# A decoder layer's attention stage on one core: a new order of steps, loads in two parts, the second norm moved and rewritten, four unread products at the seam

## The reference

```
# 1 attention with relative positions (16 heads of 8), per batch
q, k, v = x @ Wq + bq, x @ Wk + bk, x @ Wv + bv
scores  = (q k^T + c2p(q, pos_k) + p2c(k, pos_q)) / sqrt(3 * 8)
a       = softmax(scores) v @ Wo + bo
x       = layernorm(a + x) * ln_scale + ln_bias      # "first norm", eps 1e-7
# residual and a post norm around it
x       = layernorm(x_in + x)                        # "second norm", eps 1e-5
# 2 cross attention to ctx_768 (ternary weights, int8 activations), then a norm
# 3 four rounds of four experts (128 -> 512 -> 128, top 2 of 4)
# 4 a last norm
```

## Time and profile before

| | |
|---|---|
| median of 3 runs | 2843.77 us (2837.84 to 2845.44) |
| the profiled execution | 2838.59 us, of which its span 2836.9 us |
| busy over the span | PE 2414.7, DVE 2232.0, ACT 2286.8, POOL 711.7 us |
| attention stage | from 0 to about 950 us of the span |
| one body of its loop | 54.70 us |
| mean granted clock of TensorE | 0.939 of 2.4 GHz |

### The profile page before, as it was taken

One profiled execution on the slowest core, in us unless ns is written; L12 is line 12 of the kernel. 1 busy time (PEld: TensorE's weight loads), 2 busy tenths in 40 slices (PEclk: granted clock), 3 DMA queues, 4 the chain that ended last, 5 costly groups with the idle time before them and its releaser, 6 DMA issues. The chain is left out here.

```text
span 2836.9 us, 64292 instructions
## 1 busy us (share of the span) xinstructions
PE 2414.7 (85%) x18180; PEld 1323.1 (47%) x18199; DVE 2232.0 (79%) x6591; ACT 2286.8 (81%) x4255; POOL 711.7 (25%) x565
## 2 busy tenths in 40 slices
PE   2888888888888337746699999999999999999997
PEld 1555555555555226614344444444444444444443
DVE  3788888788888576785488888888888888888887
ACT  1888888888888353317699999999999999999997
POOL 2334534544444101124311111111111111111114
PEclk7899999999999659977799999999999999999999
DMA  2000000000000100000011111211111121111113
GB/s 78 13 22 12 11 17 16 11 13 20 11 11 12 44 0 1 0 30 0 16 45 53 52 45 45 60 45 45 52 52 45 45 60 45 45 53 51 45 45 89
DMA packets 182540, 96.04 MB, mean 34 GB/s; under 512 B 22539, under 2 KB 179291, under 8 KB 182491
## 3 DMA queue, kind: packets, MB, share of 16 engines
q1 hardware_dynamic: 182491, 95.45, 12.0%
HBM read 78.10 MB, written 4.73 MB: 29 GB/s over the span
## 5 line engine op out<-in xcount | busy, mean ns | idle before, releaser
L1955 DVE TENSOR_TENSOR c_Hl<-c_HF,c_Hh 128x512 f16<-128x512 f32 x1028 | 679.6, 688 | 160.9 <-ACT c_Hh L1842 144.7
L1838 ACT ACTIVATE c_HF<-c_H,c_b 128x512 f32<-128x512 f32 x1028 | 711.0, 692 | 64.2 <-PE c_H L1777 44.3
L1842 ACT ACTIVATE c_Hh<-c_H,c_b 128x512 f16<-128x512 f32 x1028 | 706.4, 687 | 0.0
L1893 POOL TENSOR_TENSOR c_EX<-c_euler,c_D 128x16 f32<-128x16 f32 x65 | 188.6, 2902 | 1194.6 <-DVE c_D L1928 1194.6
L1775 PE MATMUL c_H<-c_Ch,SH 128*128 128x512 f16 x1028 | 390.1, 379 | 0.0
L1777 PE MATMUL c_H<-c_Ch,SH 128*128 128x512 f16 x1028 | 390.0, 379 | 0.0
L1776 PE MATMUL c_H<-c_Cl,SH 128*128 128x512 f16 x1028 | 390.0, 379 | 0.0
L1786 PE MATMUL c_Y<-c_Hh,SH 128*128 128x512 f16 x1024 | 388.1, 379 | 0.3 <-DVE c_Hl L1955 0.3
L1788 PE MATMUL c_Y<-c_Hl,SH 128*128 128x512 f16 x1024 | 388.1, 379 | 0.0
L1787 PE MATMUL c_Y<-c_Hh,SH 128*128 128x512 f16 x1024 | 388.1, 379 | 0.0
L692 DVE CUSTOM_DVE_ANT_0 a_T<-a_S,a_POS 128x128 f32<-128x128 f32 x1024 | 234.8, 285 | 48.0 <-PE a_S L436 41.0
(11 more groups left out here) (300 smaller groups left out, 4372.8 us busy)
## 6 DMA issues: line engine op xcount, KB each, us to landing
c_CWB<-c_rows SPq DMA_DIRECT2D x260, 256.0 KB, 4.1
a_QN<-a_QH SPq DMA_DIRECT2D x128, 32.0 KB, 1.9
a_KN<-a_KH SPq DMA_DIRECT2D x128, 32.0 KB, 1.8
out<-d_O SPq DMA_DIRECT2D x16, 256.0 KB, 2.3
a_QN<-a_QL SPq DMA_DIRECT2D x64, 32.0 KB, 1.9
a_KN<-a_KL SPq DMA_DIRECT2D x64, 32.0 KB, 1.8
CUR<-in_ctx SPq DMA_DIRECT2D x1, 1848.0 KB
c_rows<-c_CWR SPq DMA_DIRECT2D x65, 8.0 KB, 1.4
```

Source lines behind the costliest of these rows:

```text
L1838: act.activation(HF[:, k % 4, :], bH[k % 4][:, :], ACT.Gelu_apprx_tanh, bias=b1[:, g % EXPERTS, f:f + 1], scale=1.0 / WSCALE).then_inc(hf_ ...
L1842: act.activation(Hh[:, g % 2, f, :], bH[k % 4][:, :], ACT.Gelu_apprx_tanh, bias=b1[:, g % EXPERTS, f:f + 1], scale=1.0 / WSCALE).then_inc( ...
L1955: dve.tensor_tensor(Hl[:, g % 2, f, :], HF[:, k % 4, :], Hh[:, g % 2, f, :], ALU.subtract)\
```

## The change

- Loads: x comes in three parts. The first block is on a semaphore of its own (`x_in`), SP waits for it, then come the second block, the late loads and the rest of x (`late_in`). The engines start on the early loads alone. Five of GpSimd's fills move behind its first copy (`filled`).
- The stacking DMAs signal by group: `qn_in` and `kn_in` become four semaphores each, and a bucket tile waits for its own group. Who needs all of them waits for four.
- Steps: Q stays in step 1, K goes to step 2, with `high_half` behind the exponentials and `low_half` in steps 2 and 3. V's four products go to steps 10 to 13, one each, its sum to step 14. Tile 0 goes to step 5 and tile 1 stays in step 6 (`tiles_of`).
- `unit_columns` comes ahead of the tiles' roundings on ScalarE.
- GpSimd takes the maximum of units 7 to 13 and no longer of unit 6. `residuals` waits for the first norm of the block before instead of for its second.
- The second norm goes from step 9 to step 14, and from `tensor_scalar` with two columns to `scalar_tensor_tensor`, whose second tensor is the column rstd with a step of zero.
- In the last step TensorE does four products of 128 x 512 into bO that nobody reads.

```diff
-NORM_STEPS = (2, 3, 4, 5, 6, 7, 9)
+NORM_STEPS = (2, 3, 4, 5, 6, 7, 14)
+TILE_STEPS = (5, 6, 7, 7, 8, 8, 9, 9, 10, 10, 11, 11, 12, 12, 13, 13)
+V_STEPS = (10, 11, 12, 13)
-EARLY_MAX = range(6, 14)
+EARLY_MAX = range(7, 14)
+def tiles_of(u):
+    return [n for n, step in enumerate(TILE_STEPS) if step == u]
...
-        qn_in, kn_in = Count(sem("qn_in"), 16 * 3 * NG), Count(sem("kn_in"), 16 * 3 * NG)
+        qn_in, kn_in = ([Count(sem(n + str(g)), 16 * 3) for g in range(NG)] for n in ("qn_in", "kn_in"))
...
-                for src, dst in loads + late:
+                for src, dst in loads:
                     sp.dma_start(dst, src).then_inc(loaded, 16)
+                for n in range(2):
+                    sp.dma_start(X[:, n * NB:(n + 1) * NB, :], tokens[:, n * NB:(n + 1) * NB, :]).then_inc(x_in, 16)
+                    if n == 0:
+                        sp.wait_ge(x_in, 16)
+                for src, dst in late:
+                    sp.dma_start(dst, src).then_inc(late_in, 16)
...
-            def residuals(i):
-                hold(pool, spare_pool, link_s.sem, link_s.at(i, 0))
+            def residuals(i, first):
+                if not first:
+                    hold(pool, spare_pool, link_s.sem, link_s.at(i, -3))
...
-                if n == 0:
-                    pe.wait_ge(qn_in.sem, qn_in.at(i, qn_in.per * (1 + nxt)))
-                if n == 2 * NG:
-                    pe.wait_ge(kn_in.sem, kn_in.at(i, kn_in.per * (1 + nxt)))
+                if j == 0:
+                    done = (qn_in, kn_in)[kind][g]
+                    pe.wait_ge(done.sem, done.at(i, done.per * (1 + nxt)))
...
                     if u == 1 and not last:
-                        project_qk(i, 1)
+                        project_q(i, 1)
                     if u == 2 and not last:
-                        project_v(i, 1)
+                        project_k()
+                    if u in V_STEPS and not last:
+                        project_v(V_STEPS.index(u))
...
+                    if u == UNITS + TAIL - 1 and not last:
+                        for _ in range(4):
+                            pe.matmul(bO[:, :], window[:, 0:P], table[:, 0, :, :, :].rearrange("p k j n -> p (k j n)"),
+                                      start=True, stop=True)
...
                     if 0 <= u - 3 < UNITS:
                         exp_columns(i, u - 3)
-                    for n in range(2 * (u - 6), 2 * (u - 6) + 2):
-                        if 0 <= n < TILES and not last:
-                            high_rows(i, 1, n)
                     if u >= 7 and (u - 7) % UPB == 0 and u < 7 + UNITS:
                         unit_columns(i, (u - 7) // UPB)
+                    for n in tiles_of(u):
+                        if not last:
+                            high_rows(i, 1, n)
                     if u < UNITS:
                         exponentials(i, u)
+                    if u in (1, 2) and not last:
+                        high_half(i, 1, u - 1)
...
-                    last = dve.tensor_scalar(X[:, bass.ds(i * NB + b, 1), :], R[:, b, :], mv[:, b, 0:1],
-                                             rstd[:, b:b + 1], ALU.subtract, ALU.mult)
+                    last = dve.scalar_tensor_tensor(
+                        X[:, bass.ds(i * NB + b, 1), :].rearrange("p a h -> p (a h)"), R[:, b, :], mv[:, b, 0:1],
+                        rstd[:, b:b + 1].to_broadcast([P, H]), ALU.subtract, ALU.mult)
...
-                    if u == 1 and not last:
-                        low_half(i, 1, 0)
-                        low_half(i, 1, 1)
-                    if u == 2 and not last:
+                    if u in (2, 3) and not last:
+                        low_half(i, 1, u - 2)
+                    if u == 14 and not last:
                         values_in(i, 1)
```

More of the change, by code:

```diff
@@ L333, in _ @@
             const(pool.memset(PS, 0.0))
[L334 to L338, removed]
             const(pool.memset(half[:, :], -0.5))
             assert n == CONSTS
-            pool.wait_ge(loaded, LOADS)
+            pool.wait_ge(x_in, 16)
             copy_block(0, 0)
+            pool.wait_ge(xb.sem, 1)
+            pool.memset(table[96:128, :, :, :, :], 0.0).then_inc(filled, 1)
+            pool.wait_ge(filled, 1)
+            pool.memset(QN[96:128, :, :, :], 1.0).then_inc(filled, 1)
+            pool.wait_ge(filled, 2)
+            pool.memset(KN[96:128, :, :, :], 1.0).then_inc(filled, 1)
+            pool.wait_ge(filled, 3)
+            pool.memset(V[:, :, :, :], 0.0).then_inc(filled, 1)
+            pool.wait_ge(filled, 4)
+            pool.memset(V[:, :, :, DH:DH + 1], 1.0).then_inc(filled, 1)
+            pool.wait_ge(filled, FILLS)
             pool.wait_ge(built, BUILT)
@@ L363, in body @@
                         take_max(i, u)
-                    if u == NORM_STEPS[5] and not first:
-                        power(i - 1, 1)
-                residuals(i)
+                    if u in (NORM_STEPS[1], NORM_STEPS[5]) and not first:
+                        power(i - 1, (NORM_STEPS[1], NORM_STEPS[5]).index(u))
+                residuals(i, first)
                 if not last:
@@ L386, in transposes, with project_q, project_k, project_v @@
                 last.then_inc(xT_ps.sem, 1)
-            def project_qk(i, nxt):
+            def project_q(i, nxt):
                 pe.wait_ge(xT_ok.sem, xT_ok.at(i, 1 + nxt))
                 pe.matmul(bG[0][:, :], Wq[:, :], xT[:, ::-1, :], start=True, stop=True).then_inc(qk_ps.sem, 1)
+            def project_k():
                 pe.matmul(bG[1][:, :], Wk[:, :], xT[:, :, :], start=True, stop=True).then_inc(qk_ps.sem, 1)
[L393 to L396, removed]
+            def project_v(b):
+                pe.matmul(bM[:, b * S:(b + 1) * S], xT[:, :, b], Wv[:, :], start=True, stop=True).then_inc(v_ps.sem, 1)
             def bucket_tile(i, nxt, n):
@@ L500, in _ @@
             pe.wait_ge(tab, 5)
-            project_qk(0, 0)
-            project_v(0, 0)
+            project_q(0, 0)
+            project_k()
+            for b in range(NB):
+                project_v(b)
             pe.wait_ge(tab, TAB)
@@ L626, in body @@
                         x_columns(i, 1)
-                    if u == 1 and not last:
-                        high_half(i, 1, 0)
-                        high_half(i, 1, 1)
                     if 0 <= u - 3 < UNITS:
                         exp_columns(i, u - 3)
-                    for n in range(2 * (u - 6), 2 * (u - 6) + 2):
-                        if 0 <= n < TILES and not last:
-                            high_rows(i, 1, n)
                     if u >= 7 and (u - 7) % UPB == 0 and u < 7 + UNITS:
                         unit_columns(i, (u - 7) // UPB)
+                    for n in tiles_of(u):
+                        if not last:
+                            high_rows(i, 1, n)
                     if u < UNITS:
                         exponentials(i, u)
+                    if u in (1, 2) and not last:
+                        high_half(i, 1, u - 1)
                     if u in OUT_COLS:
@@ L868, in body @@
                         norm_step(i - 1, NORM_STEPS.index(u))
-                    for k in range(2 * (u - 6), 2 * (u - 6) + 2):
-                        if 0 <= k < TILES and not last:
+                    for k in tiles_of(u):
+                        if not last:
                             split_rows(i, 1, k)
```

53 lines of the change are left out of this document (31 added, 22 removed).

## The result

The changed kernel is slower: 2872.66 us median (2870.77 to 2873.83, 4 runs) against 2844.47 us (2837.84 to 2845.44, 4 runs), a ratio of 1.0104 (95% interval 1.0086 to 1.0121). The forecast was 2793. Of the profiled execution the span is 2870.8 us, 33.9 longer than before.

What follows compares the result with a forecast made beforehand. Waits between TensorE, VectorE and ScalarE, none full, make a body's time; the prologue waits for loads. Gains 22.0 (prologue) + 28 (14 bodies) + 1 - 3 = 48 us give 2793 us, own range 2776 to 2810, for all 2774 to 2830.

Steps and rivals of the forecast that it cites:

- second rival: Step 14: GpSimd gets between the norm's instructions; one turn 2819 us (chance 0.20), two 2845 (0.05), three 2867 (0.15).
- Loads, 16.3 us: Prologue: engines wait only for early loads and x's first 256 KB; start moves from 26.14 to about 9.8 us.
- Stacking by groups, 5.7 us: Prologue: with a semaphore for each group the first bucket tile starts at 49.4, not 55.15; 5.7 us gained.
- Fills, 0: Prologue: GpSimd's five fills behind the first copy end near 19 us, well before their reader; no cost counted.
- Clock, 1.0 us a body: Seam between bodies: four unread products keep TensorE's clock up, gaining 1.0 us a body, bounds 0 and 1.2.
- Q, K and V, 1.3 us: Steps 1 to 3: VectorE loses the wait for V's products and their sum; 1.3 us gained, bounds 0.8 and 1.8.
- V's pairs, -0.5: Steps 10 to 13: V's products return as one pair a step; 0.5 us a body lost, bounds 0 and 1.5.
- Step 9, 1.1 us: Step 9: the second norm's 2.11 us leave, then ScalarE sets the pace; 1.1 us gained, bounds 0.6 and 2.
- Bank's copy, 0: Step 12: the copy ahead of the roundings releases TensorE but delays those roundings; 0, bounds -0.5 and +0.5.
- Step 14, -0.9 us: Step 14 takes in the values' sum and second norm, delaying unit 15's exponential; 0.9 us lost, bounds 0.5 and 1.5.
- Body 0, +1, and the semaphore waits, -3 in all: Body 0, without a norm, gains about 1 us; separate semaphores add waits of 0.2 us a body, 3 us.

Runs made afterwards that it cites:

- products only: The kernel before with only the four unread products added at the end of each body but the last: 2830.96 us, ratio 0.9964.
- the version with GpSimd behind the norm: Changed kernel with the count in residuals back from -3 to 0, so GpSimd waits for the second norm; norm stays in step 14: 2803.92 us, 0.9863.
- the other place: Changed kernel with the second norm ahead of the values' sum in step 14: 2868.75 us, ratio 1.0106.
- the halves: Changed kernel with GpSimd's copy of QS and its four products each in two halves: 2848.64 us, ratio 1.0022.

## Why the prediction was wrong

The step that failed is step 14 of the change, and in it the sentence that "the 0.25 is what is left of GpSimd's second residual sum when the norm begins". It looks one instruction of GpSimd ahead. That sum cost the first instruction 0.04 us (0.38 instead of 0.34). Behind it stood the copy of QS and four products. The four instructions took 4.77 us instead of 1.14 + 0.25: two of them were held for 2.1 us each. The prediction had this as its second rival, with a chance of 0.05 for the two turns that came and of 0.15 for the time that came, and weighed it by the wrong question, whether the three behind the first hold together. They don't: whichever comes up while GpSimd runs a copy lets it end (halves of copies gave halves of turns).

What decides is an edit that the prediction did not price at all: `residuals` waiting at -3 instead of 0. Before, a norm in any step held GpSimd back by itself. With that one number back, and all else as changed, 69 of the 80 us between 2873 and the forecast are gone.

The other terms, one by one:

- **Loads, 16.3 us:** 16.1. Right.
- **Stacking by groups, 5.7 us:** 9.82 - 4.10 = 5.7. Right.
- **Fills, 0:** wrong by 2.1 us. The prediction asked only when their readers want them. Three instructions of VectorE stood still beside them, two of these at the same fill.
- **First block of x, in the loads:** forecast to land at 10.1 us, it is there at 10.83, 0.8 behind VectorE's start, and TensorE waits for GpSimd's copy of it: 0.6 us. The prologue gave 18.9 instead of 22.0.
- **Clock, 1.0 us a body:** right as a mechanism and in size (10.5 us in the kernel before, 1.05 x 11 = 11.6). Of the 1.05 us, 0.6 lie ahead of the T of unit 0 (17.5 and 16.8 us from unit 15 on) and 0.4 behind it. In the changed kernel nothing was left of it: the stall of step 14 drew the clock down for longer than the seam had.

For the next terms the row to compare with is "products only", which has the full clock at the seam as the changed kernel has:

- **Q, K and V, 1.3 us:** at unit 3 the changed kernel is 2.0 us ahead; the low half of K, which is now in step 3, takes 0.7 back, and from unit 5 to unit 9 it is 1.3. Right.
- **V's pairs, -0.5:** between units 10 and 14 it loses 0.5 (10.7 and 10.2 us). Right.
- **Step 9, 1.1 us:** between units 9 and 10, 3.1 instead of 4.2. Right.
- **Bank's copy, 0:** about +0.1 a body, +0.3 with the two bodies in which the clock fell. Within its bounds.
- **Step 14, -0.9 us:** in the version with GpSimd behind the norm the exponential of unit 15 starts 3.96 us after the T of unit 14 (forecast 4.0), and from unit 14 to the next body it takes 18.8 us, where "products only" takes 18.0. That is -0.85, so the term is right once nothing of GpSimd's is in the way.
- **Body 0, +1, and the semaphore waits, -3 in all:** body 0 -0.1 in the changed kernel (52.4 and 52.3), +0.8 in the run with the norm in step 9 (51.5), although it has no norm. The two traces differ in how far the prologue's low clock reaches into it: 4.2 us behind the first T in the one (to 72.4), 2.3 in the other (to 70.4). Of the waits nothing can be seen.

The sum of a body came out at 52.6, where the clock held, against 52.7 forecast, and not by errors that cancel: 1.05 + 1.3 - 0.5 + 1.1 - 0.85 = 2.1. GpSimd's first `power` also moved, from the start of the body to step 3, which neither the list of changes nor the sum has; nothing is left over for it. That the clock would fall behind step 14 even with 3.0 us there, in 8 bodies at 1.3 us, is what keeps that version at 2804 and not at 2793.

The second rival's own arithmetic was wrong too. It priced two turns at 3.7 us and three at 5.3. Two came, and cost 5.3: 6.6 - 3.0 = 3.6 us of delay against the version without them, and 1.7 more from there to the next body (17.6 and 15.9), in which TensorE runs at half its clock. That the median came within 6 us of the time of the three turns was luck.

Not settled: that an instruction which starts in the gap of 0.19 us ahead of the copy of QS passes (the one at 330.4, and the second of the four in the two runs with the other place and with the halves) was read, not tried with other gaps; what the clock follows, as at the seams of the kernel before the same work met either level, and only that products there keep it is shown; and in which bodies the clock falls behind a gap of 3 us and in which it doesn't.

## What to carry to other kernels

When an edit loosens what an engine waits for, ask what its whole row then runs beside, not only the next instruction: here a wait that looked idle kept four cheap instructions of VectorE out of GpSimd's copies. Price a meeting of the two engines as the rest of the GpSimd instruction in progress for each VectorE instruction that comes up meanwhile, which in back-to-back rows is nearly a whole one each, and add what TensorE's clock loses in the gap. Fills and copies that are "off the path" belong where the other engine waits for something else, or behind it.

## What the runs showed of the hardware

- A held VectorE instruction waited for the one GpSimd instruction in progress and not for the next: 2.13 and 2.16 us with copies of 2.1; with copies of 1.2 the two took 1.19 each, and the row of four grew by 0.86 a turn (2.86 - 1.14 for two). GpSimd's next then gave way to it: 2.53 instead of 2.1 us behind a held `tensor_tensor` of 512 columns. `scalar_tensor_tensor`, `tensor_scalar` and `tensor_tensor` on SBUF are held alike by a copy; an operand that is read with stride zero changes nothing of that.
- Beside a fill it is otherwise: `tensor_tensor` 96x64 took 0.22 us, as it does alone, and `tensor_scalar` 96x4 took 1.22 instead of 0.16.
- In a gap of 4.27 us on TensorE in step 14 the clock fell to half and stayed there from 335.6 to 341.6 (0.55 over 7.4 us); where T of units 14 and 15 were 3.0 us apart it fell in 8 of 14 bodies. Four products of 512 columns that nobody reads kept it at 1.00 over all seams, at 11 of which it had fallen.
